# Moving four short matmul products to another PSUM ring and giving every group its own pace in a hand-timed order (decoder layer, one core)

## What is computed

```python
# _L0_attn_ref: recurrence, then a gated network; bit_linear rounds tokens to 8 bits, weights to -1, 0, 1
h = rms_norm(x, g_pre)
a = sigmoid(bit_linear(h, w_a) + decay_bias)
v = sigmoid(bit_linear(h, w_i)) * bit_linear(h, w_v)
rec_out = chunked_scan(a, sqrt(clip(1 - a*a, 1e-8)) * v)        # state = a*state + value
ffn_out = bit_linear(silu(bit_linear(rms_norm(rec_out, g_post), w_gate)), w_down)
x = layernorm(x + (x + rec_out + ffn_out))
# _L0_xattn_ref: Q from x; K, V from the context; rope on Q and K
x = layernorm(x + softmax(Q @ K.T / 4) @ V @ Wo.T + bo)
# _L0_ffn_ref: weights are +1 or -1
h = 2*relu(s0 * (concat([x, -x]) @ w0)); h = 2*relu(s1 * (h @ w1))     # 1024 wide
x = layernorm(x + s2 * (h @ w2))
```

## Time and profile before

| | us |
|---|---|
| median of 3 runs (847.07, 851.01, 849.92) | 849.92 |
| the profiled execution | 846.09 |
| its span, first to last instruction | 844.2 |
| PE busy in the span | 786.2 (93%) |
| DVE busy | 611.8 (72%) |
| ACT busy | 579.5 (69%) |
| POOL busy | 317.9 (38%) |

### The profile page before, as it was taken

One profiled execution on the slowest core, in us unless ns is written; L12 is line 12 of the kernel. 1 busy time (PEld: TensorE's weight loads), 2 busy tenths in 40 slices (PEclk: granted clock), 3 DMA queues, 4 the chain that ended last, 5 costly groups with the idle time before them and its releaser, 6 DMA issues.

```text
span 844.2 us, 18112 instructions
## 1 busy us (share of the span) xinstructions
PE 786.2 (93%) x6893; PEld 572.9 (68%) x6926; DVE 611.8 (72%) x1199; ACT 579.5 (69%) x960; POOL 317.9 (38%) x562
## 2 busy tenths in 40 slices
PE   1897768999999999999999999999999999999996
PEld 1454326677786868686867768686868777776675
DVE  5754768696978788786969687878879696857242
ACT  6665476959687786869595967778695959563622
POOL 6983225251433423453424343342434251330010
PEclk9999589999999999999999999999999999999998
DMA  9003010203020211111020302111120202020000
GB/s 306 8 26 107 13 33 4 87 2 90 14 82 22 61 42 43 61 37 55 16 86 14 89 14 71 33 58 45 39 64 15 77 14 64 14 64 14 2 13 26
DMA packets 53029, 40.69 MB, mean 48 GB/s; under 512 B 7344, under 2 KB 52432, under 8 KB 52944
## 3 DMA queue, kind: packets, MB, share of 16 engines
q1 hardware_dynamic: 52944, 39.53, 15.5%
HBM read 26.66 MB, written 12.59 MB: 46 GB/s over the span
## 4 chain that ended last, share of the span: by engine, by line
PE 84%; DVE 8%; ACT 4%; issue 2%; POOL 1%; ACTq 0%; DVEq 0%; POOLq 0%
PE bankC L1321 27%; PE bankA L1258 7%; PE bankA L1172 7%; PE bankC L1305 6%; PE bankC L1337 6%; PE bankA L1107 5%; PE slotB L1245 4%; PE slotB L1227 4%; PE slotB L1179 3%; PE bankA L1088 3%; PE bankA L1179 3%; DVE nmax L1625 2%; PE bankC L1353 2%; PE slotB L1277 2%; PE bankA L1098 2%
## 5 line engine op out<-in xcount | busy, mean ns | idle before, releaser
L1321 PE MATMUL bankC<-h0h,w 128*128 128x256 f16 x1024 | 232.4, 273 | 0.5 <-DVE h0l L1669 0.5
L1321 PE MATMUL bankC<-h0l,w 128*128 128x256 f16 x1024 | 231.8, 273 | 0.0
L1625 DVE TENSOR_REDUCE nmax<-slotB 128x4 f32<-128x1024 f32 x128 | 153.9, 1215 | 17.5 <-PE slotB L1227 17.5
L964 ACT ACTIVATE pr<-slotB,cscale 128x1024 f32<-128x1024 f32 x128 | 139.1, 1118 | 10.9 <-PE slotB L1245 10.6
L1321 PEld LDWEIGHTS bankC<-h0h,w 128*128 128x128 f16 x1024 | 100.2, 98 | 28.6 <-issue 14.1
L1321 PEld LDWEIGHTS bankC<-h0l,w 128*128 128x128 f16 x1024 | 100.2, 98 | 15.4
L1258 PE MATMUL bankA<-pr,v_aug 128*32 128x256 f32 x1024 | 69.5, 389 | 0.0
L1669 DVE SCALAR_TENSOR_TENSOR h1l<-bankC,h1h 128x512 f16<-128x512 f32 x64 | 43.5, 679 | 25.8 <-ACT h1h L994 25.6
L1305 PE MATMUL bankC<-xh,w 128*128 128x256 f16 x256 | 58.6, 273 | 1.9 <-DVE h0l L1669 1.1
L745 POOL TENSOR_TENSOR qt<-qb,turn 128x256 f32<-128x256 f32 x32 | 22.7, 730 | 98.8 <-ACT qb L918 98.8
L1337 PE MATMUL bankC<-w,h1h 128*128 128x256 f16 x256 | 59.1, 273 | 0.7 <-DVE h1l L1669 0.6
(11 more groups left out here) (253 smaller groups left out, 1779.0 us busy)
## 6 DMA issues: line engine op xcount, KB each, us to landing
x<-in_x SPq DMA_DIRECT2D x16, 256.0 KB, 2.9
cT<-in_ctxT SPq DMA_DIRECT2D x16, 256.0 KB, 3.0
scr<-kpart SPq DMA_DIRECT2D x16, 256.0 KB, 2.6
k_st<-scr SPq DMA_DIRECT2D x32, 128.0 KB
scr<-qpart SPq DMA_DIRECT2D x16, 256.0 KB, 2.3
q_st<-scr SPq DMA_DIRECT2D x32, 128.0 KB, 2.7
out<-x SPq DMA_DIRECT2D x16, 256.0 KB, 2.1
k_st<-scr SPq DMA_DIRECT2D x32, 64.0 KB
```

The costliest lines, as they stand in the source:

```text
L964: act.activation(pr[i % 2][:, c, :, :].rearrange("p h s -> p (h s)"), slotB[ringB.slot(g, name)][:, :], ACT.Exp, scale=cscale[:, g:g + 1])\
L1321: ins = pe.matmul(bankC[ringC.slot(g, name)][:, e * T:(e + 1) * T], w_1[:, i // 2, (2 * m + e) * P:(2 * m + e + 1) * P], (h0h, h0l)[i % 2] ...
L1625: dve.tensor_reduce(nmax[:, 0:H * NT].rearrange("p (a q b n) -> p q n a b", a=2, q=NHG, b=2)[:, hg, n], slotB[ringB.slot(g, name)][:, :].r ...
```

## The change

1. `max`, `oT`, `wo` and `x2T` are products of at most 512 numbers a row. They move from `slotB` to `bankA`; `oTok`, which needs 1024, stays.
2. `rotq` on DVE is cut in two steps: `rotq` keeps the multiplication, the new step `qa` does the addition, and has a place of its own in the order.
3. `when` stretches a stage about a pivot by a factor for each stage and group (`PACE`). The factor is 1 for groups 4 to 12, so only the first four and the last three groups get their own.
4. All numbers in `TIMES` and `BEGIN` are new. Counted in steps, some 173 of PE's 1098 stand elsewhere, 93 of ACT's 668, 77 of DVE's 701, 52 of POOL's 214, 41 of SP's 129.
5. `cn` on ACT waits for the one of the group before.

No product, no element-wise work and no DMA is added or taken away.

```diff
 def when(step, engine, g):
-    return BEGINS[step][g] + AT[step][engine]
+    stage = STAGE[step]
+    return BEGIN[stage][g] + PIVOT[stage] + (AT[step][engine] - PIVOT[stage]) * PACE[stage][g]
...
+PIVOT = {"weights": 0, "recurrent": 0, "keys": 35, "context": 10, "queries": 65, "scores": 90, "values": 116, "network": 145}
+PACE = {
...
+    "scores": [0.85, 1.02, 1.03, 1.059, 1, 1, 1, 1, 1, 1, 1, 1, 1, 0.974, 1.084, 1.054],
+    "values": [0.971, 0.951, 1.008, 1.033, 1, 1, 1, 1, 1, 1, 1, 1, 1, 0.973, 1.008, 0.913],
...
-           "pv0": ("ACT", "pv1"), "pv2": ("ACT", "pv3")}
-B_ITEMS = {**{f"score{u}": ("DVE", f"score{u}") for u in range(NT * NHG)}, "max": ("DVE", "max"),
+           "oT": ("ACT", "oT"), "wo": ("DVE", "wo"), "x2T": ("DVE", "x2T"), "max": ("DVE", "max"), "pv0": ("ACT", "pv1"), "pv2": ("ACT", "pv3")}
+B_ITEMS = {**{f"score{u}": ("DVE", f"score{u}") for u in range(NT * NHG)},
            **{f"exp{i}.{c}": ("ACT", f"exp{i}.{c}") for i in range(NHG) for c in range(NT)},
-           "oTok": ("DVE", "oTok"), "oT": ("ACT", "oT"), "wo": ("DVE", "wo"), "x2T": ("DVE", "x2T")}
+           "oTok": ("DVE", "oTok")}
...
-                take(g, ringB, "wo")
-                across_tokens(slotB[ringB.slot(g, "wo")], oT, w_o).then_inc(ringB.full_sem(g, "wo"), 1)
+                take(g, ringA, "wo")
+                across_tokens(bankA[ringA.slot(g, "wo")], oT, w_o).then_inc(ringA.full_sem(g, "wo"), 1)
...
                 ins.then_inc(ringA.free_sem(g, "q"), 1)
+
+            def rotated(g):
                 dve.wait_ge(*ringA.emptied(g, "q"))
                 dve.wait_ge(*qs_s.at(g))
                 dve.tensor_tensor(qt1[:, :, :], qt1[:, :, :], qt2[:, :, :], ALU.add).then_inc(qr_s.sem, 1)
```

More of the change, by code:

```diff
@@ L81 @@
-        w:tab V34.438 | w:wk G40.558 | w:wq G47.854""",
-    "recurrent": """
[L83 to L88, removed]
+        w:s V-302.832 P-10.472 | w:m V-82.877 A-38.813 P0.144 | w:a V-79.589 | w:iv V10.845
@@ new lines @@
+        w:h27 P40.077 | w:h28 P83.335 | w:h29 P47.006 | w:h30 P47.844 | w:h31 P52.831
+        w:mask V28.943 S29.384 P31.924 | w:sgn V13.952 | w:k0 V43.95 | w:k2 V26.037 | w:k1.0 A33.478
+        w:k1.1 A37.336 | w:k1.2 A38.562 | w:k1.3 A63.517 | w:rope G12.447 P14.638 A18.332
+        w:bqk P19.19 A20.407 | w:sq A17.184 P25.262 V28.738 G32.36 | w:bs G33.2 A60.694 | w:tab V33.378
+        w:wk G33.638 | w:wq G42.38""",
+    "recurrent": """
+        loadx S35.247 | scale A6.193 G-5.503 V-2.838 | stat1 G12.554 | round V13.012
+        xqT P15.769 A18.905 | iv0 P20.613 A21.454 V22.273 | iv1 P23.79 A26.541 V25.9 | a P19.291 A20.294
+        aT P23.121 A25.636 | sq A27.56 | ivT P26.901 V30.633 | cum V31.5 | recur V32.056
+        rec P33.818 A35.922 V33.395 | max2 V35.64 | stat2 G33.576 | round2 V36.667 | rqT P37.964 A41.876
+        gate0 P40.701 A45.094 V46.973 | gate1 P42.062 A45.277 V47.217 | stat3 G50.494 | round3 V48.125
+        sqT P51.168 A53.428 | down P55.03 V56.844 | bn V58.314 G68.593 | x1 V65.581""",
@@ L96 @@
[L96 removed]
+        x1T P63.889 A66.442 | xb G90.868 | q P68.183 A68.734 | rotq G73.169 V70.323 | qa V71.594
+        qp A76.099 V74.882 | qput S44.983 | qget S51.584""",
     "scores": """
[L98 to L100 removed]
+        score0 P88.33 V90.541 | score1 P90.299 V91.079 | score2 P90.72 V94.359 | score3 P92.926 V97.378
@@ L101 @@
+        score4 P98.128 V100.433 | score5 P98.719 V100.508 | score6 P104.055 V106.054
+        score7 P104.082 V109.473 | max P112.282 A115.368 V115.2 | maxrow S84.953""",
     "values": """
[L102 to L105, removed]
@@ L106 @@
-        bn2 V141.116 G149.518 | x2 V145.874""",
-    "network": """
[L108 to L115, removed]
+        exp0.0 P117.598 A119.694 | exp0.1 P117.721 A120.404 | pv0 P121.231 | exp1.0 P119.969 A122.536
@@ L138, in times @@
 def times():
-    table, begin = {}, {}
+    table, stage_of = {}, {}
     for stage, text in TIMES.items():
```

138 lines of the change are left out of this document (73 added, 65 removed).

## The result

| | before | changed |
|---|---|---|
| median, us | 850.12 (847.07 to 851.01, 4 runs) | 842.33 (839.26 to 842.84, 4 runs) |
| ratio, 95% interval | 1 | 0.9904 (0.9880 to 0.9928) |
| the profiled execution, and its span | 846.09, 844.2 | 839.26, 837.5 |

What follows compares the result with a forecast made beforehand. PE's own work bounds the middle; in the head PE waits for chains through other engines. Terms 0.5 - 1.1 - 4.0 + 0.3 - 0.6 + 0.5 = -4.4 us: 841.7 profiled, 845.5 median; range 840 to 852.

Steps and rivals of the forecast that it cites:

- A: Head, weights and group 0, 37 to 62 us: POOL's `stat2` before `cn` and `cg` delays `gate0`; +0.5 us.
- B: Head, `x1` of group 0 to `rqT` of group 1: `round` fits into DVE's wait for POOL; -1.1 us.
- C: Head, scores of group 0 to `m_lo`: DVE no longer waits for ACT's `iv` gates; -4.0 us, bounds -3.4 and -4.4.
- D: Head, `m_lo` to `rec` of group 2: ACT's reordered steps nearly cancel; +0.3 us, bounds -1.0 and +1.2.
- E: Head, `rec` of group 2 to `xl` of group 0: mainly `bn` of group 2 moved behind `xl`; -0.6 us.
- the sign of being wrong: Forecast is wrong if `xl` comes less than 2 us earlier, or the middle's idle time changes by more than 3 us.
- The rival by which POOL would not be held: First half of Rival 3: POOL not held through `w:k0`, `cg` ends near 44, A is -1.5; whole rival's chance 0.21.
- the ring: In E, transposed products take `bankA`, whose earlier users are long done: costs 0, and +1 us if not.
- F: Middle, 13 groups: `rqT` loses 0.2 us each, +2.6; `gate0` may gain, -2.1; +0.5 us, bounds -3 and +3.
- The tail: Drain after the last scores: same steps in nearly the same order; 0 us, ±0.5.
- Rival 1: Middle pays for new neighbours on ACT, `rqT` waiting a whole exponential more: 14.3 us, time 859.3; chance 0.13.
- Rival 3: Head gains more, -6.8 us, 843.1; or (second half) the middle keeps 2.1 us and loses no 2.6, 842.9; chance 0.21.

Runs made afterwards that it cites:

- e10: The changed kernel with ACT's last exponential (`exp3.1`) put back behind `pv1` in groups 1 to 15, group 0 left as it is: 839.30 us, ratio 0.9895.
- e11: e10 plus e6's wait of the first half of `w:k0` on DVE for POOL's `cn` and `cg`: 836.95 us, ratio 0.9865.
- e6: The changed kernel with the first half of `w:k0` on DVE waiting until POOL has done `cn` and `cg` of group 0: 839.87 us, ratio 0.9878.
- e5: The changed kernel with ACT's last exponential (`exp3.1`) put back behind `pv1` in all groups: 841.68 us, ratio 0.9909.
- e7: The changed kernel with POOL's `cn` and `cg` of group 0 ahead of `stat2` again, as before the change: 840.98 us, ratio 0.9901.
- e9: The kernel before, with group 0's `score7`, `x1` of group 1 and `iv1` of group 2 moved on DVE, and `max` on PE and ACT: 849.91 us, ratio 1.0012.
- e12: e9 with ACT's `sq` of group 2 ahead of `q` of group 1, and group 0's first exponential ahead of `qp`: 849.72 us, ratio 1.0014.
- e3: The kernel before in its old order throughout, with the changed kernel's new rings: 872.68 us, ratio 1.0275.
- e4: The changed kernel in its new order, with `max`, `oT`, `wo` and `x2T` back in the ring of two-bank buffers: 856.88 us, ratio 1.0089.

## Why the prediction was right, and where its steps were not

The outcome, faster, and the range held; the size was 4.4 against 7.8. Up to `xl` the terms A to E sum to -4.9 us, and -4.04 was measured, but in an execution with a higher clock than most. The clock as a gain of its own is not in the sum: e10, with the same order there and the clock of before, has -1.3, less than the 2 us that the prediction named as the sign of being wrong. So the head's total came out near the forecast partly by luck. That a us at `xl` is a us of the span holds where the rest is the same: e10 to e11, 2.27 and 2.3.

- **A**, +0.5 forecast: +0.38 at `x1` of group 0, with `gate0` 0.34 later than before where 1.1 was forecast: POOL's `cg` slipped by 3.8 us, not 4.4, since `w:wk` ended 1.0 earlier, which the sum left out. The mechanism was right and e6 shows it. By the Trainium skill (SBUF — State Buffer, "Who interferes with whom") a DVE instruction with two inputs in SBUF holds the shared port against GpSimd's reads; the 2.40 us that became 0.27 agree. The rival by which POOL would not be held is out.
- **B**, -1.1: A and B together were forecast at -0.6, and `rqT` of group 1 came 0.66 earlier (83.48 to 82.82).
- **C**, -4.0: 15.92 us from the first maximum to the end of `m_lo`, forecast 15.97, and 16.1 to 16.5 in e5, e6, e7, e10 and e11, inside the bounds (-3.4 to -4.4). The size is right; that C is worth it by itself isn't. e9 and e12 made most of it in the old order (2.4 and 3.3 us), and the end did not move.
- **D**, +0.3: 0.0 in the profiled execution. In e5, e6, e7, e10 and e11 the same stretch took 15.8 to 16.9 us instead of 14.5 (from the start of `m_lo`), with `q` of group 1 wholly or partly at half clock; there it is 1.3 to 2.4 longer than before, past my upper bound.
- **E**, -0.6: +0.7 (20.47 to 21.16 us), with waits of 0.5 to 1.1 us on PE in other places and two new ones of 0.6 on DVE; in e6, e7, e10 and e11 it is 21.9 to 22.7. That the ring "costs 0 here" holds in the old order (e3, the old order with the new rings, has 20.53). In the new order it is the old rings that cost: e4 needs 26.7 us for the same stretch, partly at half clock.
- **F**, +0.5: this is the term that was mis-sized; -2.0 measured. `rqT` loses 0.28 a group (forecast 0.2). The -2.1 for `gate0` was an error: its delay is 0.22 us in both kernels. In 6 of 11 middle groups it now stands behind a network product, where no wait is listed (0.33 us to its start instead of 0.11), in the other 5 still behind `pv3` (1.23 instead of 1.01). What did bring the gain was left out, the other products that got new neighbours.

  Summed from start to start of PE's rows over 11 middle groups: network products ahead of `rqT` +3.1; `wo` and `kT` -2.2 (8 matmuls, 1.83 us to the next start before, 1.73 now; `v` has 1.73 in both); scores -1.7, and network products ahead of them -1.7 (0.20 us instead of 0.11, 28 times before, 10 times now); the rows of L1098 -1.2; all others +1.2; together -2.45. `kT` had a score behind it before and has none now. Why `wo`, in another ring but ahead of the same step, is 0.1 us shorter wasn't tested, nor was any of these neighbours moved by itself: this account is read off two traces.

  I had taken PE's idle time, 0.29 us in a window of 48, as all that an order could win there; the list is blind to gaps that a modelled end covers. The Trainium skill (Perfetto Trace Analysis, "Tensor Engine Instruction (MATMUL, LD_WEIGHTS)") says that the end of a matmul in a profile is estimated, and the 0.39 us between two starts with no idle time listed agree.
- The tail, forecast 0 ± 0.5: -0.71, outside its bounds.

Rival 1, the middle paying for its new neighbours, had its sign right at `rqT` but a quarter of its price. Rival 3's second half (the middle keeps 2.1) has the right sum by the wrong account.

## What to carry over

In the head, compare traces at a like granted clock, and look at the clock of all executions: here it was two thirds of what the trace of the head gained. A ring of buffers and a fixed order are one decision: here each alone costs 8 to 23 us and both together gain 8, so neither half of such a change should be judged, or kept, without the other. On PE, price hand-overs by the distance of starts against the usual slot, not by listed idle time. Where a tiny GpSimd instruction takes microseconds, look at what DVE runs beside it, and let the long DVE instruction wait for the short chain.

## What was not expected of the hardware

The same order meets the two clock levels at different places from one execution to the next, and in the head that is worth 3 us. The changed kernel's profiled execution had a mean granted clock of 0.99 and took 839.26 us; its others, at 0.981 to 0.983, took 842.2 to 842.8. e6's fastest, 836.59, was at 0.992, its slowest, 840.73, at 0.981. The places can be seen where two traces share the order: the head of the changed kernel and that of e10, 0.95 and 0.89 up to `xl`. The rows below are the transposed maxima and `q` of group 1, in the changed kernel and in e6, whose PE stood idle as long (1.68 us) before the maxima:

```profile
100.47 0.30 PE L1251 MATMUL bankA<-ident,nmax 128*128 128x128 f32 x1 [1.68 <-DVE iv L1520]
...
103.00 1.97 PE L1187 MATMUL bankA<-x1T,w_q 128*128 128x256 f32 x8
```
```profile
98.03 0.45 PE L1251 MATMUL bankA<-ident,nmax 128*128 128x128 f32 x1 [1.68 <-DVE iv L1521]
...
101.38 3.45 PE L1187 MATMUL bankA<-x1T,w_q 128*128 128x256 f32 x8
```

At 1.2 GHz it holds the first exponentials' product back by 1.5 us and, with the steps ahead of it, by 2. A milestone of the head compared between single traces therefore carries an error of that size, the group step of the middle does not: 45.99 in three traces, 45.76 in three others.
